# Vision tower kernel on one core: input pieces, number of warm-up products, and width of two weight loads

## The reference, cut to what matters

```
h = patches @ tok_Wp.T + tok_bp                                  # embedding, 768 -> 192
h = layernorm(h + attention(h, w_qkv, window 65, 12 heads) @ w_out + b_out)
h = layernorm(h + experts(h, Wqk, Wv, conv, glob, gates) @ ffn_Wp + ffn_bp)
```

## Time and profile before

| what | value |
|---|---|
| median of 3 runs | 114.96 us (114.75 to 116.04) |
| the profiled execution, its own time | 115.59 us |
| its span, first to last instruction | 113.8 us |
| PE busy | 104.5 us, 92% of the span |
| PE weight load busy | 93.7 us, 82% |
| DVE busy | 76.7 us, 67% |
| ACT busy | 72.2 us, 63% |
| POOL busy | 21.5 us, 19% |
| moved by DMA | 7.73 MB |

### The profile page before, as it was taken

The page is one execution under the profiler, slowest core; times in us unless marked ns, Lnnn a source line. Parts: engine busy times, 40 slices in busy tenths (PEclk is TensorE's granted clock), DMA queues, the critical chain, the costliest instruction groups (busy, mean ns, idle before and its releaser), DMA issues.

```text
span 113.8 us, 3528 instructions
## 1 busy us (share of the span) xinstructions
PE 104.5 (92%) x1381; PEld 93.7 (82%) x1381; DVE 76.7 (67%) x240; ACT 72.2 (63%) x200; POOL 21.5 (19%) x34
## 2 busy tenths in 40 slices
PE   6999999999999999999999999999969878978940
PEld 4699899997799989799988998999958777876920
DVE  0565909276935787249585978887767779988661
ACT  4577784588898775946954378762366468539260
POOL 7003624554156500000493000000000000000000
PEclk9999999999999999999999999999999999999998
DMA  3999999200000000000000000000000000000202
GB/s 75 333 347 402 411 418 424 84 0 6 3 0 6 3 0 6 0 6 0 0 0 6 0 0 6 6 0 0 0 3 6 3 0 6 0 0 0 64 19 78
DMA packets 4124, 7.73 MB, mean 68 GB/s; under 512 B 1293, under 2 KB 2445, under 8 KB 3981
## 3 DMA queue, kind: packets, MB, share of 16 engines
q1 hardware_dynamic: 3740, 7.24, 17.6%
q10 hardware_dynamic: 368, 0.28, 0.7%
HBM read 7.08 MB, written 0.44 MB: 66 GB/s over the span
## 4 chain that ended last, share of the span: by engine, by line
PE 65%; DVE 16%; DMA 5%; issue 5%; ACT 3%; SPq 3%; DVEq 0%
PE proj L933 11%; PE score L1014 8%; PE outp L1059 7%; DMA x_f<-x_t 5%; PE outp L897 5%; PE proj L918 4%; PE trans L1038 4%; PE proj L925 3%; PE proj L919 3%; PE proj L922 3%; PE proj L926 3%; DVE wqk_f L759 2%; DVE ln_st L744 2%; ACT ln_ln L566 2%; SPq L375 1%
## 5 line engine op out<-in xcount | busy, mean ns | idle before, releaser
L545 ACT ACTIVATE pt_t<-trans,image_t 108x216 f32<-108x216 f32 (+1 forms) x42 | 14.6, 425 | 3.7 <-PE trans L1038 3.3
L1014 PE MATMUL score<-k_t,q_t 64*36 64x37 f32 (+1 forms) x416 | 10.5, 196 | 0.0
L1014 PEld LDWEIGHTS score<-k_t,q_t 64*36 64x36 f32 x416 | 9.0, 111 | 1.6 <-issue 1.0
L529 ACT ACTIVATE score<-d_t 128x296 f32<-128x296 f32 (+2 forms) x16 | 6.6, 413 | 5.8 <-DVE d_t L708 5.8
L705 DVE TENSOR_REDUCE mx_t<-score 128x8 f32<-128x296 f32 (+2 forms) x16 | 7.1, 444 | 4.5 <-PE score L1022 4.2
L718 DVE TENSOR_REDUCE sm_t<-score 128x8 f32<-128x288 f32 (+1 forms) x16 | 7.0, 438 | 4.2 <-ACT score L529 4.2
L566 ACT ACTIVATE ln_ln<-ln_mv,const 108x1 f32<-108x1 f32 (+1 forms) x12 | 3.6, 297 | 8.6 <-DVE ln_mv L747 8.6
L657 DVE TENSOR_TENSOR x_lo<-x_f,x_hi 128x288 fp32r<-128x288 f32 x12 | 6.3, 534 | 4.0 <-ACT x_hi L461 4.0
L505 ACT ACTIVATE q_t<-proj 128x288 f32<-128x288 f32 x12 | 5.0, 417 | 6.2 <-PE proj L926 5.9
L933 PE MATMUL proj<-wv_hi,h_hi 128*108 128x384 f32 (+1 forms) x24 | 8.2, 343 | 0.0
L418 POOL TENSOR_TENSOR wqk_lo<-wqk_f,wqk_hi 128x256 fp32r<-128x256 f32 x6 | 4.5, 756 | 18.1 <-ACT wqk_hi L465 18.1
(11 more groups left out here) (208 smaller groups left out, 341.5 us busy)
## 6 DMA issues: line engine op xcount, KB each, us to landing
ffn_f<-f_w SPq DMA_DIRECT2D x1, 1088.0 KB, 12.2
wqk_f<-w_qk SPq DMA_DIRECT2D x2, 512.0 KB, 8.2
x_f<-x_t SPq DMA_DIRECT2D x2, 432.0 KB, 6.5
wv_f<-w_v SPq DMA_DIRECT2D x1, 768.0 KB, 7.4
wo_f<-w_out SPq DMA_DIRECT2D x1, 768.0 KB, 9.9
x_f<-x_t SPq DMA_DIRECT2D x2, 288.0 KB, 4.8
tw_f<-tok_w SPq DMA_DIRECT2D x2, 256.0 KB, 4.6
wqk_f<-w_qk SPq DMA_DIRECT2D x2, 256.0 KB, 5.9
```

The costliest lines, as they stand in the source:

```text
L545: nc.scalar.activation(pt_t[:, n % 2, 0:tiles, :, i], trans[0:ROWS, 0:tiles, :, 0:TOK], ACT.Copy, scale=image_t[:, i:i + 1]).then_inc(spli ...
L1014: ins = nc.tensor.matmul(s[64 * h:64 * h + TOK, im, 0:width], q, k_t[rows, n % QK_RING, im, 0:width], start=(kind == "attn" and im == 0), ...
```

## The change

The third and fourth chunk of the first group's inputs, and of the embedding weights, each get a transfer of their own, so that there are five pieces instead of four. `SP_TOK` becomes (2, 3, 4), so SyncE issues eight transfers ahead of the biases (five of inputs, three of weights) where it issued six. The warm-up has 16 products. The out weights and expert weights are kept and loaded without the 64 padded columns: `wo_f` 6 x 192, `ffn_f` 2 x 1024 columns. The DRAM arrays stay as they were. The lists of steps stay as they were.

```diff
-F_END = F_PROJ + DUP
+F_END = F_PROJ + DIM
 
-X_PIECES = [slice(0, 1), slice(1, 2), slice(2, 4), slice(4, 6)]
+X_PIECES = [slice(0, 1), slice(1, 2), slice(2, 3), slice(3, 4), slice(4, 6)]
...
-WARM_UP = 20
-ACT_TOK, SP_TOK = (0, 1), (2, 3)
+WARM_UP = 16
+ACT_TOK, SP_TOK = (0, 1), (2, 3, 4)
...
-        wo_f = sb("wo_f", [128, PAIRS, DUP])
-        wo_hi = sb("wo_hi", [128, PAIRS, DUP], F32R)
-        wo_lo = sb("wo_lo", [128, PAIRS, DUP], F32R)
+        wo_f = sb("wo_f", [128, PAIRS, DIM])
+        wo_hi = sb("wo_hi", [128, PAIRS, DIM], F32R)
+        wo_lo = sb("wo_lo", [128, PAIRS, DIM], F32R)
...
-            sp.dma_start(wo_f[:], w_out).then_inc(ld_wo, 16)
-            sp.dma_start(ffn_f[:], f_w).then_inc(ld_ffn, 16)
+            sp.dma_start(wo_f[:], w_out[:, :, 0:DIM]).then_inc(ld_wo, 16)
+            sp.dma_start(ffn_f[:], f_w[:, :, 0:F_END]).then_inc(ld_ffn, 16)
```

## The result

The changed kernel takes 116.2 us (median of 20 executions, 115.27 lowest) where the kernel before takes 115.31 (20 executions, 114.75 to 116.04). The ratio is 1.0059, interval 1.0041 to 1.0077: slower by 0.5 to 0.9 us. One of the twenty executions of the changed kernel took 143.61 us at a granted clock of 0.65 and is left out of the ratio, which compares executions at the usual clock. The forecast was 114.8, within 114.1 to 115.7. The sign was wrong and the time lies outside the range.

The account below looks back on a forecast made before the run. TensorE's list from em 6 was taken to set the end, its start waiting for L378's landing; between 0 (landing binds) and 0.46 us (TensorE binds) it took 0.15: 114.96 - 0.15 = 114.8 us, range 114.1 to 115.7.

Parts of the forecast that it names:

- What bounds the kernel: From 11.6 to 80 us TensorE's list sets the end; its start, em 6, waits for L378's input piece.
- The warm-up: TensorE's start: four products fewer start em 0 at 5.17; clock rise stays at 6.95, so 0.46 us gained by em 5.
- Rival C: TensorE's start: the clock stays low longer, +2.2 us, 117.2 us; chance 0.03.
- The five pieces: First group's loads: chunk 2 comes earlier, making the 0.46 us whole, by at most 0.15; SyncE's later transfers issued 0.95 later.
- So I take its landing as unmoved.: L378, second group's first input piece: issued at 5.45 instead of 4.50, yet lands as before behind the same bytes.
- chunks 4 and 5: First group's last inputs: same bytes ahead as before; x_lo of chunk 5 ready at 9.81, wanted at 10.04.
- Rival A: SyncE's queue: its 0.95 us reach L378's piece, em 6 starts later; 115.4 to 115.9 us; chance 0.15.
- Rival B: Ordinary runs: L378's piece lands some 0.5 us or more earlier, TensorE binds; 114.5 or 114.3 us; chance 0.22.
- The 192 columns: Out and expert weights: 0.4 us of ACT and 0.9 of POOL saved off the path; between 0 and -0.1 us.
- The price of rows and of more transfers: DMA: one-chunk rows hardly dearer than two-chunk rows, and the fixed part of transfers is paid in parallel.
- The rule on larger transfers: Skill page on DMA: about 2.0 us fixed per transfer, 1 MiB each asked; paid serially, two more would cost 4 us.
- The level: Base of the forecast time: 114.96 us, the median of the runs shown, with the profiled execution at 115.59.

Follow-up runs that it names:

- w16: Kernel before with 16 warm-up products instead of 20, nothing else changed; ratio 1.0009 (0.9984 to 1.0033).
- before_order: Kernel before with one wait more: POOL starts the first weight pair's second-half remainder only once x_lo of chunk 6 is written; ratio 0.9977 (0.9952 to 1.0001).
- act_issue: Kernel before with five pieces, the weights of pieces 2 and 3 issued on ACT's queue instead of SyncE's; ratio 1.0006 (0.9983 to 1.0029).
- bias_late: Kernel before with the biases' transfer moved behind L378; ratio 0.9981 (0.9958 to 1.0005).
- tok_split_only: Kernel before with only the embedding weights in five pieces, the inputs in four; ratio 1.0045 (1.0023 to 1.0066).
- combo: Changed kernel with weight pieces 2, 3 on ACT's queue, biases behind L378, second-group inputs in two and four chunks, hh 0, hl 0 before xs 8; ratio 0.9984.
- early_delay: Kernel before with two 16-byte transfers on SyncE's queue ahead of piece 2; ratio 1.0072 (1.0047 to 1.0098).
- after_order: Changed kernel with one wait more: POOL starts the first weight pair's second-half remainder only once x_lo of chunk 6 is written; ratio 1.0043 (1.0019 to 1.0067).
- after_look2: Changed kernel, nothing altered, profiled a second time; that execution took 116.05 us.
- delay4: Kernel before with four 16-byte transfers on SyncE's queue ahead of the biases, behind all first-group transfers; ratio 1.0032 (1.0009 to 1.0056).
- cols192: Kernel before with the 192-column loads of out and expert weights alone; ratio 1.0020 (0.9996 to 1.0044).

## Why the prediction was wrong, point by point

**What bounds the kernel** was right in its first half. From em 6 on the end follows its start: span less the start of em 6 is 101.9 to 102.6 us in all twenty profiles, for starts from 10.89 to 12.78. That the start follows the landing of L378's piece is so where the piece is late. In w16, before_order, act_issue, bias_late, tok_split_only and combo, with landings up to 10.33, em 6 comes right behind em 5.

**The warm-up.** em 0 was forecast at 5.17 and started at 5.23, em 5's last product at 10.75 (forecast 10.70 by its start), and the spacing of products fell to 0.13 us near 6.75. That the rise of the clock would stay at 6.95 was luck. Read from the spacing, it comes at 3.7 us in early_delay and after_order, 4.7 in w16, 6.2 in after_look2 and 7.1 in before_order, with TensorE at work without a break since 1.07 in each. It moves by over 3 us between executions in which TensorE did the same up to then, so 0.46 us was never a fixed price of four products. Where the clock rises early, TensorE comes to em 2 before chunk 2 is there, and the products saved turn into waiting. w16, 1.0009, shows the outcome: the warm-up alone gives nothing. Rival C falls, since no profile has the slower spacing beyond 7.1 us.

**The five pieces, the step that failed.** It read: "So I take its landing as unmoved." Two premises stood under it. That L378's own issue at 5.45 comes in time was nearly true: delay4 issues it at 5.65, lands it at 10.25 in its profile and costs 0.3%. That the engines are full, the bytes ahead are the same and so the landing is the same was not: 11.0 us instead of 10.4 in the mean of the profiles above. I checked the queue for the one transfer on the chain and not for the pieces ahead of it, which are themselves issued later, and just where the engines had the fewest bytes ahead of them. There one-chunk pieces come at 293 GB/s, and 276 to 297 GB/s are moved instead of 332. The busy share of 1.05 in the earlier trace rows had told me there was no room; it is 0.96 to 1.03 with a tenth fewer bytes moved. GB/s is the column to read. The same premise stood under chunks 4 and 5 ("the same bytes stand ahead of them as before"). In the kernel before ACT takes up chunk 4's inputs at 8.11 without waiting for them; in the three profiles of the changed kernel it waits for them until 8.15, 8.27 and 8.77, and em 5's last product starts at 10.75, 10.89 and 11.39. In the last of these the warm-up's gain is gone before L378 comes into it.

**Rival A** named the right place and price (0.4 to 0.95 us on top of the kernel before; measured 0.9 above its median of 115.31) with the wrong condition, and got 0.15. It ought to have been the forecast: the one row in which the chain's own step moved by 0.95 us was SyncE's. **Rival B** was half right: landings some 0.3 to 0.4 us earlier than profiled do occur (10.33, 10.33 and 10.21 in w16, cols192 and before_order), and in w16 and before_order TensorE binds em 6. The gain that it drew from this doesn't show (w16).

**The 192 columns** were put at 0 to -0.1 us; 1.0020 (0.9996 to 1.0044) allows 0 and a small loss; -0.1 us would be 0.9991, just outside.

**The price of rows and of more transfers** was right: act_issue has all of them and 1.0006. The rule on larger transfers, weighed there, would have had the right sign, yet for a reason that act_issue excludes.

**The level.** The forecast stood on the median of three, 114.96, where twenty give 115.31. That is 0.35 us of its miss of 1.4.

## What to carry to other kernels

When transfers are split or added on one queue, compare the bytes issued so far with the bytes moved so far for each transfer from the first on, not only for the one that ends the chain; a gap ahead of it reaches it through the queue. Splitting cost nothing here once a second queue took four of the weights' issues (1.0006 and 0.9996). And set the profiled execution's time beside the median before believing its rows: here the one profile showed the forecast come true in a kernel that is slower.

## What the runs showed of the hardware that I had not expected

A transfer of one chunk takes SyncE's queue 0.48 us, one of 16 bytes 0.30 us. The Trainium skill (DMA: Bandwidth & Descriptors, Rules for kernel authors) says that spreading transfers over issuing engines doesn't help bandwidth and only saves issue time; here that issue time was on the path, 1.0093 with one queue and 1.0006 with two for the same transfers.

A delay of some 0.6 us on SyncE's queue cost 0.3% behind the first group's transfers and 0.7% ahead of its third piece, and doubling the one behind added nothing (1.0030 and 1.0032).

The DMA engines' busy share stood at 0.96 to 1.03 in the changed kernel while they moved 285 to 297 GB/s, and at 1.04 with 332 in the kernel before. Why a tenth fewer bytes fill the same share is not shown.

The clock's rise moved between 3.7 and 7.1 us over the twenty profiles, with TensorE at work from 1.07 us on in all.

VectorE and GpSimd, starting 0.05 to 0.07 us apart, settle which of them takes 0.3 to 0.5 us longer; where it is VectorE, TensorE's long stretch starts later.
